# Decoder layer on one core: first batch prepared in quarters with rows copied directly, value bias folded into the output bias

## The reference

```python
qkv = layernorm(x) @ qkv_w.T + qkv_b                  # 16 heads of 16 columns
scores = q @ k.T / 4 - |i - j| * 0.5 ** head          # 1024 x 1024 for each head
x = x + (softmax(scores) @ v) @ out_w.T + out_b
x = x + (q2 + softmax(ctx_queries @ keys.T / 16) @ values) @ Wo.T + bo   # 77 context rows, q2 = layernorm(x)
x = x + mixture(layernorm(x))                          # 8 experts, top 2, 256 -> 1024 -> 256
```

## Time and profile before

| | |
|---|---|
| median of 3 runs | 1537.01 us (1536.56 to 1537.97) |
| the profiled execution, its own time | 1541.59 us |
| its span | 1539.7 us |
| TensorE matmul busy | 1481.3 us (96%) |
| VectorE busy | 1172.5 us (76%) |
| ScalarE busy | 1014.2 us (66%) |
| GpSimd busy | 415.0 us (27%) |
| mean granted TensorE clock | 0.981 |
| chain that ended last, by engine | PE 84%, DVE 8%, issue 3%, ACT 3% |

### The profile page before, as it was taken

How to read it: one execution, slowest core, us unless ns; L and a number is a source line. 1 busy time by engine, 2 the same in 40 slices (tenths; PEclk the granted TensorE clock), 3 DMA queues, 4 the chain that set the end, 5 groups by cost and what they waited for, 6 DMA issues and landing times.

```text
span 1539.7 us, 28797 instructions
## 1 busy us (share of the span) xinstructions
PE 1481.3 (96%) x9670; PEld 890.0 (58%) x9670; DVE 1172.5 (76%) x2578; ACT 1014.2 (66%) x1826; POOL 415.0 (27%) x457
## 2 busy tenths in 40 slices
PE   5899999999999999999999999999999999999997
PEld 3433443244444334444443444335999999999996
DVE  5889887788887778888877877854778887665563
ACT  3056666677655757665567575778677788776673
POOL 3200130002110014211003210023537655544453
PEclk9799999999999989999989999999999999999998
DMA  5750350330432504205042230133568888899993
GB/s 143 129 120 13 45 121 34 41 43 4 66 71 55 97 22 77 35 9 124 29 69 55 44 43 10 48 121 127 165 190 230 259 234 240 240 269 260 255 269 79
DMA packets 90404, 172.55 MB, mean 112 GB/s; under 512 B 14467, under 2 KB 48515, under 8 KB 90256
## 3 DMA queue, kind: packets, MB, share of 16 engines
q1 hardware_dynamic: 73120, 142.98, 37.0%
q0 software_dynamic: 15744, 26.54, 8.4%
q10 hardware_dynamic: 1392, 1.18, 0.4%
HBM read 134.27 MB, written 36.00 MB: 111 GB/s over the span
## 4 chain that ended last, share of the span: by engine, by line
PE 84%; DVE 8%; issue 3%; ACT 3%; DMA 1%; SPq 1%; POOL 0%; ACTq 0%; POOLq 0%; DVEq 0%
PE ps L1257 15%; PE ps L1231 15%; PE ps L1217 12%; PE ps L1459 4%; PE ps L1478 4%; PE ps L1479 3%; PE ps L1457 3%; PE ps L1458 3%; PE ps L1480 3%; DVE sums L1683 2%; PE ps L1363 2%; PE ps L1329 2%; PE ps L1220 2%; PE ps L1461 2%; PE ps L1276 1%
## 5 line engine op out<-in xcount | busy, mean ns | idle before, releaser
L1503 ACT ACTIVATE prob<-ps 128x512 f32<-128x512 f32 x1024 | 562.4, 606 | 305.2 <-PE ps L1217 175.0
L1257 PE MATMUL ps<-stacked_k,stacked_q 112*128 112x512 bf16 x1024 | 396.4, 393 | 17.1 <-DVE rmax L1683 4.0
L1683 DVE CUSTOM_DVE_ANT_0 sums<-ps,ramps 128x512 bf16<-128x512 f32 x480 | 328.9, 685 | 81.3 <-PE ps L1257 73.8
L1685 DVE TENSOR_REDUCE rmax<-ps 128x1 f32<-128x512 f32 x480 | 327.3, 687 | 73.7 <-PE ps L1257 69.3
L1217 PE MATMUL ps<-stacked_q,stacked_k 115*128 115x512 bf16 x1024 | 363.4, 384 | 4.2 <-ACT prob L1503 1.8
L1257 PEld LDWEIGHTS ps<-stacked_k,stacked_q 112*128 112x128 bf16 x1024 | 100.2, 99 | 334.8 <-DVE rmax L1683 117.7
L1231 PE MATMUL ps<-prob,values 128*32 128x512 f32 x2048 | 275.5, 610 | 1.3 <-issue 0.8
L2128 POOL DMA_INDIRECT out<-yo,token_of x71 | 139.6, 1966 | 189.8 <-DVE yo L2010 138.8
L1634 ACT ACTIVATE hid<-ps,w_now 128x256 f32<-128x256 f32 (+1 forms) x312 | 124.7, 452 | 88.3 <-PE ps L1459 59.6
L1217 PEld LDWEIGHTS ps<-stacked_q,stacked_k 115*128 115x128 bf16 x1024 | 99.8, 98 | 100.4 <-ACT prob L1503 53.9
L1478 PE MATMUL ps<-w_high,hid_high 128*128 128x256 f32 x512 | 149.1, 291 | 1.5 <-DVE sums L2004 1.5
(11 more groups left out here) (246 smaller groups left out, 2399.4 us busy)
## 6 DMA issues: line engine op xcount, KB each, us to landing
w_now<-in_w SPq DMA_DIRECT2D x78, 514.0 KB
w_now<-in_w SPq DMA_DIRECT2D x78, 512.0 KB
stacked_q<-parts_of_rows SPq DMA_DIRECT2D x90, 128.0 KB, 6.3
stacked_k<-parts_of_rows SPq DMA_DIRECT2D x90, 128.0 KB, 6.8
xi<-expert_rows SPq DMA_DIRECT2D x71, 130.0 KB, 3.0
parts_of_rows<-q_part SPq DMA_DIRECT2D x21, 256.0 KB, 5.6
parts_of_rows<-k_part SPq DMA_DIRECT2D x21, 256.0 KB, 5.7
b_now<-in_b SPq DMA_DIRECT2D x39, 128.0 KB
```

Of the source, the lines that this page charges most:

```text
L1257: m = e.matmul(ps[:, bank, :], qa[i][0:MAX_ROW, hh, qt * P:(qt + 1) * P], ka[i][0:MAX_ROW, hh, kc * BANK:(kc + 1) * BANK], start=True, sto ...
L1503: e.activation(prob[:, u % NPROB, :], ps[:, score_bank(u), :], ACT.Exp, scale=SLOPE ** (k[0] % NG * HG + k[3])).then_inc(sem["exp"], 1)
L1683: e.tensor_tensor_reduce(sums_16[:, :], of, ramp_beside(1 - qt % 2, qt % 4), 1.0, -3.0e38, ALU.add, ALU.max, into).then_inc(sem["maxed"], 1)
L1685: e.tensor_reduce(into, of, AX.X, ALU.max).then_inc(sem["maxed"], 1)
```

## The change

It has five parts.

1. **Order of the opening.** The first four tiles of x go alone through statistics, root and norm; two of them are normed by ScalarE and two by VectorE (`normed`). The other four come after. Weights are loaded in three pieces, piece 0 right behind the first half of x; identity, scales and bias come through ScalarE's queue. All low parts of the weights are made on VectorE. TensorE starts with 14 + 5 products of zeros (`warm`), the five behind the first `aggr`.
2. **Direct rows.** The parts of the first group are copied from the split tiles to the stacks in one SBUF to SBUF DMA for each block, 24 of 64 KB in all, each as soon as its part is made. The five with the high and mid queries of column half 0 are issued by GpSimd, the others by SyncE. Group 1's 12 blocks go the same way. Heads are interleaved in the weight columns on the host (`by_group`), so 64 adjacent rows hold a group. Position rows are made in bf16 on the host and loaded directly.
3. **Maxima of group 0.** The context products join at half of the maxima, their loads go through SyncE's queue behind group 1's rows, and no maximum is placed while `placing` runs.
4. **Values** are copied by ScalarE without a bias, one instruction for a bank. `bias_fold` multiplies bv with the output weights (two products on TensorE), and `bias_made` adds the result to bo_all, once.
5. Costs in the planner's table are changed to match.

```diff
-FIRST_ALONE = 3 * UNITS // 4
+FIRST_ALONE = UNITS // 2
+FIRST_BY_ACT = 2
+DIRECT = 2.8
+WARM, WARM_AFTER = 14, 5
+def by_pool(a, n, ch):
+    return a == 0 and n < 2 and ch == 0
     def prepare_first():
...
+        add("aggr", "pre", 0, FORE)
+        add("rstd", "pre", 0, FORE)
+        add("scale_q", 0)
+        add("scale_bias")
+        add("w_high", 0)
+        add("w_low", 0)
+        add("shift", "pre", 0, FORE)
+        for tt in range(*FORE):
+            add("norm" if tt < FIRST_BY_ACT else "normed", "pre", 0, tt)
         for c in range(DC):
+            add("x_turn", 0, c, 0)
+            add("x_high", 0, c, 0)
+        for tt in range(*AFT):
+            add("stats", "pre", 0, tt)
+        for c in range(DC):
+            add("x_low", 0, c, 0)
+        add("aggr", "pre", 0, AFT)
+        add("rstd", "pre", 0, AFT)
+        add("specials")
+        for a in range(2):
+            for i in range(p.parts(("proj",))):
+                p.add_part(i, "proj", 0, 0, a, 0)
+            for n, kind in enumerate(("high", "rest", "mid", "low")):
+                add(kind, 0, 0, a, 0)
+                if kind != "rest":
+                    add("direct", a, n - (n > 0), 0)
...
+    def rows_in():
+        return p.emptied.get(("low", 0, 0, 1, int(now["maxima"] >= UNITS // 4)), float("inf")) + DIRECT
...
-        while (bank_free() and now["maxima"] < UNITS + LEAD and now["spread"] > now["maxima"] // UNITS
-               and p.pe >= rows_in[now["maxima"] >= UNITS // 4]):
+        while (bank_free() and not placing and not p.open and now["maxima"] < UNITS + LEAD and now["spread"] > now["maxima"] // UNITS
+               and p.pe >= rows_in()):
...
+        def direct_rows(e, a, n, ch):
+            cols, part = slice(ch * BANK, (ch + 1) * BANK), ("high", "mid", "low")[n]
+            if (a, n) == (1, 0) and ch == 0:
+                e.wait_ge(sem["k_ones"], 1)
+            rows = "early_rows" if by_pool(a, n, ch) else ("first_rows", "spread0")[ch]
+            e.wait_ge(sem[part], p.upto(part, 0, 0, a, ch))
+            for j, pair in enumerate(PAIRS):
+                if pair[a] == n:
+                    e.dma_start((qa, ka)[a][0][DH * j:DH * (j + 1), :, cols], split[n][a][first_group, 0, cols]).then_inc(sem[rows], 16)
...
+                elif kind == "values":
...
+                    e.activation(vt[b % 2][:, 2 * two:2 * two + 2, 0:NH * VW].rearrange("p t (h d) -> p t h d", h=NH)[:, :, :, 0:DH],
+                                 ps[:, p.bank("vproj", *k), :].rearrange("p (t h d) -> p t h d", t=2, h=NH), ACT.Copy).then_inc(sem["values"], 1)
...
+                    for c in range(DC):
+                        m = e.matmul(ps[:, bank, 0:D], bv_of[:, c:c + 1].broadcast_to([P, P]), wo[:, c, :], start=(c == 0), stop=(c == DC - 1))
```

More of the change, by code:

```diff
@@ L226, in fills @@
     def fills(self, step):
-        if step[0] in EMPTIED and step not in self.place and step[0:2] != ("x_turn", 0):
+        if step[0:2] == ("x_turn", 0):
+            self.holder[self.bank(*step)] = step
+        elif step[0] in EMPTIED and step not in self.place:
             ring = self.ring(step)
@@ L448, in complete @@
         mine = users["done"]
+        if b == 0:
+            yield from room()
+            add("bias_fold")
+            add("bias_made")
         for tt in range(*tiles):
@@ L672, in step_on @@
             parts.pop(0)
-    now = {"unit": 0, "ended": 0, "spread": 0, "maxima": 0, "running": False, "late": False}
+    now = {"unit": 0, "ended": 0, "spread": 1, "maxima": 0, "running": False, "late": False}
     placing, closing, staging, emptying, scattering = [], [], [], [], []
@@ L692, in bank_free @@
         before = p.holder.get(p.max_bank(place // UNITS, place))
-        return before is None or p.emptied["maxed", *before[1:]] <= p.pe + 0.1
+        return before is None or p.emptied.get((EMPTIED[before[0]], *before[1:]), float("inf")) <= p.pe + 0.1
     opening = prepare_first()
[L696 to L701, removed]
+    next(opening)
     now["late"] = True
@@ L1095, in _ @@
                     if G == 1:
-                        e.wait_ge(sem["positions"], 32)
-                        e.wait_ge(sem["spread0"], spread_in(0))
-                        e.wait_ge(sem["context_in"], 8 * 16)
                         for other in range(1, NSET):
                             position_rows(other)
+                        for part in ("high", "mid", "low"):
+                            e.wait_ge(sem[part], p.upto(part, 0, 0, 1, NCH - 1))
+                        for j, pair in enumerate(PAIRS):
+                            for a, rows in enumerate((qa, ka)):
+                                e.dma_start(rows[1][DH * j:DH * (j + 1), :, :], split[pair[a]][a][next_group, 0, :]).then_inc(sem["spread1"], 16)
+                        continue
                     for j, (of_q, of_k) in enumerate(PAIRS):
@@ L1189, in _, with warm @@
         def _(e):
+            def warm(n):
+                for _ in range(n):
+                    e.matmul(ps[:, AV_BANK, :], sums_16[:, 0:P], sums_16[:, :], start=True, stop=True)
+            e.wait_ge(sem["first_set"], 1)
+            warm(WARM)
+            e.wait_ge(sem["aggr"], 1)
+            warm(WARM_AFTER)
             def side_bank(*step, first=True):
@@ L1285, in _ @@
                     for q in range(4):
+                        if c == 0 and not b:
+                            by = "norm" if ("norm", "pre", 0, 4 * four + q) in p.number else "normed"
+                            e.wait_ge(sem[by], p.upto(by, "pre", 0, 4 * four + q))
                         m = e.transpose(ps[:, bank, q * P:(q + 1) * P], xr_next[:, 4 * four + q, c * P:(c + 1) * P], ident[:, :])
@@ L1512, in _ @@
                     which, b, tt = k
[L1513 removed]
+                    halved = b == (0 if which == "pre" else NB - 1)
+                    tiles = (FORE, AFT)[tt // 4] if halved else WHOLE
                     if tt == tiles[0]:
```

272 lines of the change are left out of this document (135 added, 137 removed).

## The result

The kernel after takes 1541.85 us (median of 19 runs, 1537.97 to 1546.98); the kernel before, on the same chip, 1537.04 (19 runs, 1534.67 to 1540.85). The ratio is 1.0033 (95% interval 1.0025 to 1.0041): about 5 us slower, where 13.6 faster was forecast. The profiled execution took 1540.18 us, span 1538.4, clock 0.981.

A forecast was written before the change was run, and what follows sets the result against it. TensorE was taken to bound the kernel from 200 us on, the opening being the exception. First score -14.5, + 1.0 + 0.3 - 0.4 = -13.6 us, gave 1523.4 us against the median of 1537.0; range 1515 to 1531.

The forecast's parts named there:

- What the opening bounds: Whole kernel: time taken off the first score comes off the end, the stretch behind it changing by at most 3 us.
- Until the first maximum: Start of the opening: first row maximum at 21.7 us instead of 35.06, 13.4 earlier, bounds 19.5 and 25.
- While VectorE sets the pace: Group 0's 32 maximum reductions: 4 us of gaps (bounds 1 and 9), ending at 71.6 instead of 83.8 us.
- rows or context late: Rival, opening: loads late in SyncE's queue hold back maxima, 6 to 8 us more gaps, result 1530; chance 0.15.
- TensorE waits for the context loads: Sign in the profile after, opening: if TensorE waits for these loads, the prediction is wrong.
- To the first score: Last maximum to first score: 5.6 to 5.8 us, 2.3 less; first score at 77.4 instead of 91.9.
- What comes back: Around the first score: two or three fewer group 1 maxima done, 1.0 us lost (0.6 to 2.1); `bias_fold` 0.3.
- Values: Batches 1 to 3, value copies moved from VectorE to ScalarE: 0.4 us gained, bounds 3 gained and 8.3 lost.
- GpSimd's copies held up: Rival, early direct rows: five GpSimd copies lose 2.5 us each, first maximum at 34, result 1531.5; chance 0.05.
- Slower by the half clock: Rival, opening: TensorE at half clock becomes the bound, first score near 110, +18 us, 1556; chance 0.05.

The follow-up runs named there:

- experiment 4: Kernel after with context loads ahead of group 1's rows, next batch's x loaded early, other x load held behind the maximum rows: 1530.17 us, ratio 0.9952.
- experiment 1: Kernel after with the eight context loads issued ahead of group 1's position rows and rows: 1533.28 us, ratio 0.9987.
- experiment 10: experiment 4 with maxima of group 0 allowed between the two halves of a projection again: 1529.32 us, ratio 0.9945.
- experiment 2: Kernel after with GpSimd's two 1 MB loads of x held until group 0's three maximum rows have landed: 1538.58 us, ratio 1.0009.
- experiment 5: Kernel before with the values part alone (ScalarE copies without bias, bias_fold and bias_made once): 1533.12 us, ratio 0.9979.
- experiment 6: Kernel after with its values part alone undone, bias added on VectorE again, no bias_fold: 1549.42 us, ratio 1.0052.
- experiments 9: Kernel after without the 19 warm-up products: 1543.51 us, ratio 1.0023.

## Why the prediction was wrong

**What the opening bounds.** Right, as far as medians can be joined with the first score of one trace each. Before it is 1537.0 - 91.9 = 1445.1 us from the first score to the end. For every kernel run, its ratio times 1537.0 less its first score lies between 1440.5 and 1446.1 (after 1542.1 - 97.2 = 1444.9, experiment 4 1529.6 - 84.4 = 1445.2). What moves the first score moves the end, and from the kernel before to the kernel after the stretch behind it changes by 0.2 us, inside the bound of 3 that I had set.

**Until the first maximum** (forecast 21.7, bounds 19.5 and 25; measured 26.57). Wrong by 4.9 us, outside the bounds. The step that failed is its first sentence, statistics end at 4.95 as before: they ended at 8.05, which is 3.1 of the 4.9. The second quarter of x landed at 7.28, since the broadcast of the scale, now issued at 1.19 beside it, took the DMA engines; the root began at 8.85 and not at 5.6. TensorE was not warm: transposes took 2.16 us, projections stood 0.43 apart. Together q's low part came at 19.71 and not 15.1. Then SyncE's seven issues cost 0.66 each and not 0.46:

```profile
18.00 3.02 POOL L1088 DMA_DIRECT2D stacked_q<-q_part  x5
...
20.57 3.76 SPq L1088 DMA_DIRECT2D stacked_k<-k_part  x6
...
26.57 0.65 PE L1315 MATMUL ps<-stacked_k,stacked_q 112*128 112x512 bf16 x1
```

The last of them starts near 23.7, and the direct copies land in 2.6 us (median), below the 2.9 to 3.7 taken. TensorE's second block of projections ends at the same moment, so earlier rows alone would have gained nothing: a second limit that I had not looked for.

**While VectorE sets the pace** (forecast 4 us of gaps, bounds 1 and 9; measured 16.5). This is the term that turned the sign. I had named the cause as a rival, rows or context late, and had the 36 issues behind one another in it; but I priced them at 0.46 us each and 3 us of landing, which gave 46 us. Measured are a start at 27.5 where I had 26, 24.5 us until the last of the 36 is issued where I had 17, and 10.4 us of landing where I had 3. That makes 62.4. Of the 24.5, the first 16 issues took 12.0 where 0.46 each make 7.4, since the direct copies of the second half are issued only as their parts are made; the twelve row copies took 7.7, 0.64 apart. The rival's mechanism was right, and its price of 6 to 8 us was right for this wait (experiment 1: 7.1). Its chance of 0.15 was too small, because the last load's time came from an issue rate alone, with no term for the 1.5 MB of row copies in front of it. "TensorE waits for the context loads" was also one of the signs that I had named for a wrong prediction. But that wait is only 6.5 of the 12.5 us of gaps that I had not forecast. Experiment 1 leaves 10.0, experiment 4 8.2 and experiment 10 6.2, with maxima between the halves of a side product; what makes up the rest is not shown.

**To the first score** (forecast 5.8 us from the last maximum, measured 97.18 - 87.45 = 9.7). Half right: the stretch to the first issue shrank by 2.4 as said. What failed is 3.56 from the first issue to the score: it is 7.55, as two loads of x have moved ahead of it. The prediction named the move of the context loads from GpSimd's queue to SyncE's, but did not follow what was left on GpSimd's queue: `fetch_next` behind a `fetch` that waits. Worth 3.7 us (experiment 2). The three misses, 4.9, 12.5 and 3.9, make 21.3; 19.8 of them reached the first score, 97.2 where 77.4 was forecast.

**What comes back.** Before, eight maxima of group 1 (four instructions of each of two kinds) were reduced ahead of the first score; in the kernel after seven, in experiment 4 six. One or two fewer, where two or three were forecast. The stretches behind the first score differ by 0.2 us or less from the one before, so the runs can't size the term. The products of `bias_fold`, taken as 1.0 us at most, took 1.03.

**Values.** Forecast 0.4 gained for batches 1 to 3, bounds 3 gained and 8.3 lost; on the kernel before 3.2 are gained (experiment 5), 2.8 of them behind the first score, the good end. In the kernel after (experiment 6) the stretch behind the first score is 1444.7 us without this part and 1444.9 with it: nothing gained there. So the small number was too low for the one kernel and not shown wrong for the other.

**The rivals.** Late context happened. GpSimd's copies held up did not: five issues in 3.02 us, the longest 0.77, while VectorE did rests, casts and low parts from 17.72 on. The Trainium skill's page "SBUF — State Buffer" (section "A bandwidth-pool intuition that's wrong (but worth ruling out)") has a DMA issued by GpSimd grow from about 620 to about 3100 ns beside a VectorE copy; that did not show here. The other side of the meeting did, in experiments 9 and 10, as a cast of 1.96 and 2.08 us beside a memset. Slower by the half clock was not the reason. From 27 to 56 us the granted clock was 0.99. From 62 to 70 us, right behind the wait for the context loads, it was 0.58, and four context products took 2.42 us where the next four took 1.27; but the kernel before has 2.41 there as well. The low 0.66 from 84 to 100 us follows TensorE's waits, it doesn't make them. That stage does cost something: the first score's product took 0.61 instead of 0.38.

**The sign.** I gave slower 0.05, and let it hang on the clock alone. The slower result is two plain queue effects of one and the same kind, 7.1 and 3.7 us, on top of 4.9 us missed at the start.

## What to carry to other kernels

When a change brings a stage forward, list every load that the stage needs and ask whether it comes forward too: here the context's last weight was issued at the same 52 us as before, but it landed at 62.4 and not at 56.1, and the first context step had moved from 68.6 to 56.5. Look also at what a wait counts: here a transpose waited for a weight that it doesn't use. Give the landing of a load a term for the bytes in flight ahead of it, and not only the issue time. And when a step is moved off an in-order queue, follow what remains on that queue: what stood behind a short step may now stand behind a long wait, and come out just where a small, urgent copy is due.

## What the runs showed of the hardware

Twelve copies of 128 KB from SBUF to SBUF, issued 0.64 us apart, kept the 16 DMA engines about full (107% of their time by the profile) while 124 GB/s were moved, and took 8.5 to 8.8 us to land (medians). That is half of the 235 to 270 GB/s that the same profile shows in the expert stage, with the engines busy at 0.8 to 0.9. The two differ in more than the source (a row copy writes 16 partitions, a weight load 128), so the runs don't say which of it makes the half. Three small copies in another queue than two 1 MB loads took 6.2 us to land behind them, and 1.9 when the loads were held until they had landed. One broadcast load of 128 KB delayed a 256 KB quarter of x by 2.4 us. A cast on VectorE that takes 0.43 us took 1.96 and 2.08 when it began within 0.12 us after a memset of 1.80 us on GpSimd. And SyncE issued a 64 KB direct copy in 0.6 us, where six issues of before took 0.46 each.
